# A gated-expert sum and a top-k attention laid over each other in one line of sixteen tiles

## The reference

```python
# end of block 0, _L0_ffn_ref: two gated experts' outputs of each token, projected and added
g = a * jax.nn.sigmoid(b)                       # 512 wide, per expert
eo = jnp.einsum('bth,dh->btd', g, Wo) + bo
out = out + eo * comb[..., e:e + 1]
...
# block 1, _L1_xattn_ref: 77 keys, 4 heads, the 32 largest scores of each
scores = jnp.einsum('bthd,bghd->bhtg', Q, K) / np.sqrt(DH).astype(np.float32)
topv, topi = jax.lax.top_k(scores, K_TOP)
probs = jax.nn.softmax(topv, axis=-1)
attn = jnp.zeros_like(scores).at[bi, hi, ti, topi].set(probs)
attn_mean = attn.mean(axis=1)
c_t = jnp.einsum('btg,bgd->btd', attn_mean, V)
x = layernorm(x_text, g_norm_in, b_norm_in)
scale_in, shift_in = jnp.split(c_t @ W_film_in + b_film_in, 2, axis=-1)
# x * (1 + scale) + shift (FiLM, mod_gate within) goes into a convolution over time (s4d), a second FiLM, a feed-forward network
```

## Time and profile before

| | |
|---|---|
| median of three runs | 844.28 us (844.15 to 856.82) |
| the profiled execution, its own time | 840.17 us |
| its span, first to last instruction | 838.1 us |
| busy share of the span | PE 81%, DVE 67%, POOL 46%, ACT 36% |
| mean granted TensorE clock | 0.905 of full speed |
| stage C | 398.2 to 594.8 us |
| gated sums start (their transposes) / top-k starts | 416.1 / 459.3 us |

### The profile page before, as it was taken

One profiled execution on the slowest core, in us unless ns is written; L12 is line 12 of the kernel. 1 busy time (PEld: TensorE's weight loads), 2 busy tenths in 40 slices (PEclk: granted clock), 3 DMA queues, 4 the chain that ended last, 5 costly groups with the idle time before them and its releaser, 6 DMA issues.

```text
span 838.1 us, 10777 instructions
## 1 busy us (share of the span) xinstructions
PE 677.0 (81%) x3380; PEld 378.6 (45%) x3380; DVE 564.4 (67%) x1711; ACT 303.2 (36%) x654; POOL 389.4 (46%) x450
## 2 busy tenths in 40 slices
PE   4779698449899999985898568767996999999971
PEld 2434455424354545442486223323442464657651
DVE  4868874667975656510677889988775595744266
ACT  2555564204546555510122535545211311031210
POOL 4979674037887879721102467886200120212020
PEclk9999998559999999988799779978897999999996
DMA  8920011202222222221980000200100000000003
GB/s 223 390 77 1 0 57 36 75 26 77 75 78 75 78 75 77 75 70 38 313 315 25 1 0 2 100 2 1 50 1 0 1 0 1 1 0 1 1 0 100
DMA packets 33087, 52.78 MB, mean 63 GB/s; under 512 B 8718, under 2 KB 21582, under 8 KB 32776
## 3 DMA queue, kind: packets, MB, share of 16 engines
q1 hardware_dynamic: 28040, 36.76, 13.1%
q0 software_dynamic: 4992, 15.34, 5.4%
HBM read 36.62 MB, written 15.47 MB: 62 GB/s over the span
## 4 chain that ended last, share of the span: by engine, by line
PE 44%; DVE 30%; POOL 9%; ACT 7%; issue 6%; DMA 2%; POOLq 1%; SPq 0%; DVEq 0%; ACTq 0%
PE ps L469 40%; DVE arena L1519 5%; DVE arena L2015 4%; POOL arena L1351 3%; DVE arena L2012 3%; POOL arena L1357 2%; DVE arena L335 2%; DVE kp L1519 2%; ACT L1145 1%; DVE arena L1871 1%; DVE arena L1522 1%; DVE arena L1525 1%; DVE arena L1622 1%; ACT arena L988 1%; DVE X L1525 1%
## 5 line engine op out<-in xcount | busy, mean ns | idle before, releaser
L469 PE MATMUL ps<-arena 64*32 64x32 f32 (+10 forms) x2344 | 495.8, 399 | 26.0 <-DVE arena L1808 8.7
L469 PEld LDWEIGHTS ps<-arena 64*32 64x32 f32 (+7 forms) x2344 | 233.7, 155 | 220.0 <-issue 171.4
L988 ACT ACTIVATE arena<-ps 128x512 f32<-128x512 f32 (+4 forms) x252 | 121.1, 493 | 283.3 <-PE ps L469 144.3
L330 POOL TENSOR_SCALAR rstd<-mv 128x1 f32<-128x1 f32 (+2 forms) x30 | 13.0, 434 | 234.4 <-DVE mv L324 183.4
L1871 DVE TENSOR_TENSOR arena<-ps,arena 128x512 f32<-128x512 f32 x39 | 26.9, 689 | 85.4 <-ACT arena L1145 77.4
L1400 POOL DMA_INDIRECT scr_g<-arena,destU x39 | 48.8, 1250 | 44.1 <-DVE arena L1871 35.3
L1391 POOL DMA_INDIRECT arena<-scr_z,idsU x39 | 49.5, 1270 | 22.8 <-PE ps L705 11.5
L2015 DVE MATCH_REPLACE8 arena<-arena 128x77 f32<-128x77 f32 x256 | 54.1, 222 | 0.0
L1145 ACT ACTIVATE arena<-ps 128x512 f32<-128x512 f32 x39 | 23.3, 598 | 83.6 <-PE ps L469 83.5
L1351 POOL TENSOR_TENSOR arena<-arena 128x616 f32<-128x616 f32 x32 | 40.2, 1257 | 20.7 <-DVE arena L1624 19.1
L1283 ACT ACTIVATE arena<-ps,b1p 128x512 f32<-128x512 f32 x32 | 22.0, 687 | 75.9 <-PE ps L469 75.9
(11 more groups left out here) (206 smaller groups left out, 1011.4 us busy)
## 6 DMA issues: line engine op xcount, KB each, us to landing
arena<-in_w1t SPq DMA_DIRECT2D x8, 1024.0 KB, 14.1
arena<-scr_g SPq DMA_DIRECT2D x8, 1024.0 KB, 7.9
X<-in_x SPq DMA_DIRECT2D x2, 1024.0 KB, 6.5
scr_z<-arena SPq DMA_DIRECT2D x4, 512.0 KB, 2.8
arena<-in_c_dftf SPq DMA_DIRECT2D x1, 2048.0 KB, 16.2
arena<-in_L_xattn_W SPq DMA_DIRECT2D x2, 1024.0 KB, 6.3
out<-X SPq DMA_DIRECT2D x16, 128.0 KB, 1.8
scr_k<-arena SPq DMA_DIRECT2D x4, 256.0 KB, 8.2
```

Of the source, the lines that this page charges most:

```text
L469: return pe.matmul(o, l, r, start=first, stop=final)
L988: return a.activation(o, i, ACT.Copy)
```

## The change

Parts 2 and 3 of stage C become one line. Six tiles (LEAD = 6) of the gated sums go ahead; then the attention of tile n runs together with the sum of tile n + 8, the turned sum of n + 7 and the projection of n + 6, on every engine.

What moves and changes:
- The first half of the gated sum (a scale per row) goes from VectorE to ScalarE (`half_sum`); loads come in eight pieces of two tiles in place of four of four, on four semaphores. Four of the eight are issued before the loads of the kernel rows and the Fourier table (KL, DF), four after them.
- The normalisation to U goes from VectorE to ScalarE, with mean and root combined to a bias (`nmrC`) on GpSimd, four tiles at a time.
- ScalarE also takes the exponentials of the rest `Rk`. TAKEN gives zero there, so all minus rest is the top 32. GpSimd does this subtraction, the scaling, and the sum of the four heads in two additions; VectorE's compare and reduce go away. `attn_ready` now comes from GpSimd.
- ScalarE scales the FiLM product by the root on its way out of PSUM (two copies of 256 in place of one of 512), and GpSimd's separate scale of U goes away.
- Banks: turned u, scores, projection, turned weights and FiLM product have one bank each in place of two for most. The turned sum keeps two.
- Input spectra go two per step in steps 11 to 14, in two banks. The bias additions to X come two per step in steps 8 to 15.

```diff
--- before.py
+++ after.py
...
+LEAD = 6
...
+        HALF = NSEL * 2 * HID0
+        yg = [Region(at).take(NSEL, 2, HID0) for at in
+              (0, HALF, keep_k + NT * D, keep_k + NT * D + HALF, keep_kl + 2048, keep_kl + 2048 + HALF, keep_k + NT * D + HALF)]
+        yg.append(kpf[:, 0:HALF].rearrange("p (a b c) -> p a b c", a=NSEL, b=2))
...
-                sp.wait_ge(s["gy0"], 32)
                 load_gated(2)
-                sp.wait_ge(s["gy1"], 32)
-                sp.wait_ge(s["sum_ready"], 4)
                 load_gated(3)
                 sp.wait_ge(s["k_out"], 64)
                 load(sp, KL, scr_k.rearrange("(k p) n -> p k n", p=P), "k_in")
                 load(sp, DF, d["c_dftf"].rearrange("(k p) n -> p k n", p=P), "dft_in")
+                for i in (4, 5):
+                    sp.wait_ge(s[f"gy{i - 4}"], 32)
+                    load_gated(i)
+                sp.wait_ge(s["gy3"], 32)
+                load_gated(7)
+                sp.wait_ge(s["gy2"], 32)
+                sp.wait_ge(s["sum_ready"], 8)
+                load_gated(6)
...
+                def out_B(T):
+                    pe.wait_ge(s["sumT_sb"], T + 1)
                     if T:
...
+                        pe.wait_ge(s["xB_done"], T)
+                    for f in range(4):
+                        ins = mm(ps[:, 4, 0:D], GT[:, T % 2, f, :], wof[:, f, :], f == 0, f == 3)
+                    ins.then_inc(s["oB_ps"], 1)
...
+                def film_in(n):
+                    pe.wait_ge(s["AT_sb"], n + 1)
+                    if n:
+                        pe.wait_ge(s["film_sb"], n)
+                    mm(bank(6), AT[0:BIAS_ROW + 1, n * P:(n + 1) * P], VW[0:BIAS_ROW + 1, n // TB, 0, :], True, True)\
+                        .then_inc(s["film_ps"], 1)
...
+                for T in range(LEAD + 1):
+                    turn_sum(T)
+                    if T:
+                        out_B(T - 1)
                 pe.wait_ge(s["prepC_v"], 7)
...
                 turn_u(0)
                 turn_u(1)
                 scores(0)
...
+                for n in range(NT + 1):
+                    if n + 1 < NT:
+                        scores(n + 1)
+                    if n + LEAD + 1 < NT:
+                        turn_sum(n + LEAD + 1)
+                    if n + LEAD < NT:
+                        out_B(n + LEAD)
+                    if 1 <= n <= 8:
+                        kernel_spectrum(n - 1)
+                    if n == 11:
+                        pe.wait_ge(s["sd_ready"], 2)
+                        pe.wait_ge(s["dfx_in"], 16)
+                        pe.wait_ge(s["ks_done"], 8)
+                    if 11 <= n <= 14:
+                        for i in (2 * (n - 11), 2 * (n - 11) + 1):
+                            if i >= 2:
+                                pe.wait_ge(s["xf_sb"], i - 1)
+                            spectrum(i // 2, i % 2, (5, 4)[i % 2])
+                    if n:
+                        turn_attn(n - 1)
+                    if n + 2 < NT:
+                        turn_u(n + 2)
+                    if n:
+                        film_in(n - 1)
...
+                def half_sum(T):
+                    i = T // 2
+                    a.wait_ge(s[f"gy{i % 4}"], 32 * (i // 4 + 1))
+                    if T >= 2:
+                        a.wait_ge(s["sumT_ps"], T - 1)
+                    a.activation(G[:, T % 2, :], yg[i][:, 0, T % 2, :], ACT.Copy, scale=cw[:, 0, T:T + 1])\
+                        .then_inc(s["gated_half"], 1)
...
+                def exp_top_and_rest(n):
+                    a.wait_ge(s["top_full"], n + 1)
+                    for h in range(H1):
+                        ins = a.activation(topx[:, n % 2, h, :], top[:, n % 2, h, :], ACT.Exp, bias=smC[:, n % 2, 3, h:h + 1],
+                                           accum_out=smC[:, n % 2, 0, h:h + 1])
+                    ins.then_inc(s["ex_sum"], 1)
+                    for h in range(H1):
+                        R_ = Rk[:, n % 2, h * S2:(h + 1) * S2]
+                        ins = a.activation(R_, R_, ACT.Exp, bias=smC[:, n % 2, 3, h:h + 1])
+                    ins.then_inc(s["rest_exp"], 1)
...
+                def put_film(n):
+                    a.wait_ge(s["film_ps"], n + 1)
+                    a.wait_ge(s["lnC_rstd"], 2 * (n // 4) + 2)
+                    if n >= 2:
+                        a.wait_ge(s["xin_ready"], n - 1)
+                    a.activation(filmS[:, n % 2, 0:D], bank(6, D), ACT.Copy, scale=rstd[:, TB + n:TB + n + 1])
+                    copy(filmS[:, n % 2, D:2 * D], ps[:, 6, D:2 * D]).then_inc(s["film_sb"], 1)
...
+                for T in range(LEAD + 1):
+                    put_sumT(T)
+                    half_sum(T + 2)
+                    if T == LEAD - 1:
+                        norm_u(0)
                 put_uT(0)
                 put_uT(1)
                 put_scores(0)
                 for n in range(NT + 1):
                     if n < NT:
...
+                        exp_all(n)
+                    if n + 1 < NT:
+                        put_scores(n + 1)
+                    if n + LEAD + 1 < NT:
+                        put_sumT(n + LEAD + 1)
+                    if n + LEAD + 3 < NT:
+                        half_sum(n + LEAD + 3)
+                    if 11 <= n <= 14:
+                        put_spectrum(2 * (n - 11))
+                        put_spectrum(2 * (n - 11) + 1)
+                    if n in (2, 6, 10):
+                        norm_u(n // 4 + 1)
+                    if n < NT:
+                        exp_top_and_rest(n)
+                    if 1 <= n <= 8:
+                        put_kernel(n - 1)
                     if n:
...
+                        put_attn(n - 1)
+                    if n + 2 < NT:
+                        put_uT(n + 2)
+                    if n:
+                        put_film(n - 1)
...
+                def weights(n):
+                    q_, E = smC[:, n % 2], Ex[:, n % 2, :]
+                    p.wait_ge(s["ex_sum"], n + 1)
+                    own.done(p.tensor_tensor(q_[:, 1, :], q_[:, 0, :], negone[:], ALU.pow))
+                    own.settle()
+                    own.done(p.tensor_scalar(q_[:, 2, :], q_[:, 1, :], tmask[:, n:n + 1], None, ALU.mult))
+                    p.wait_ge(s["rest_exp"], n + 1)
+                    own.done(p.tensor_tensor(E, E, Rk[:, n % 2, :], ALU.subtract))
+                    own.settle()
+                    hE = E.rearrange("p (h k) -> p h k", h=H1)
+                    own.done(p.tensor_tensor(hE, hE, q_[:, 2, :].unsqueeze(2).broadcast_to([P, H1, S2]), ALU.mult))
+                    own.settle()
+                    own.done(p.tensor_tensor(E[:, 0:2 * S2], E[:, 0:2 * S2], E[:, 2 * S2:SW], ALU.add))
+                    own.settle()
+                    if n >= 2:
+                        p.wait_ge(s["AT_ps"], n - 1)
+                    p.tensor_tensor(a77[:, n % 2, :], E[:, 0:S2], E[:, S2:2 * S2], ALU.add).then_inc(s["attn_ready"], 1)
+                def x_in(n):
+                    p.wait_ge(s["film_sb"], n + 1)
+                    F_, o = filmS[:, n % 2, :], XIN[:, n - n % 4 + XSLOT[n % 4], :]
+                    own.done(p.tensor_tensor(F_[:, 0:D], F_[:, 0:D], U[:, n, :], ALU.mult))
+                    own.settle()
+                    p.tensor_tensor(o, F_[:, 0:D], F_[:, D:2 * D], ALU.add).then_inc(s["xin_ready"], 1)
...
+                for n in range(NT + 2):
+                    if n in (2, 6, 10):
+                        rstd_u(n // 4 + 1)
+                    if n >= 2:
+                        x_in(n - 2)
+                    if 1 <= n <= NT:
+                        weights(n - 1)
+                    if n == 10:
                         p.wait_ge(s["ks_ps"], 8)
                         p.wait_ge(s["xin_ready"], TB)
                         for i, kind in enumerate((ALU.add, ALU.subtract)):
                             p.tensor_tensor(SD[:, i], *folded(0), kind).then_inc(s["sd_ready"], 1)
...
+                def add_B(T):
+                    v.wait_ge(s["oB_ps"], T + 1)
+                    v.tensor_tensor(X[:, T, :], X[:, T, :], ps[:, 4, 0:D], ALU.add).then_inc(s["xB_done"], 1)
+                    v.wait_ge(s["xB_done"], T + 1)
+                    own.done(v.bn_stats(bstat[:, T % TB, :], X[:, T, :]))
...
+                sum_gated(0)
+                sum_gated(1)
+                film_rows()
+                for T in range(LEAD):
+                    sum_gated(T + 2)
+                    add_B(T)
+                for n in range(NT):
+                    top_eight(n, 0)
+                    top_eight(n, 1)
+                    if n + LEAD + 2 < NT:
+                        sum_gated(n + LEAD + 2)
+                    top_eight(n, 2)
+                    if 2 <= n <= 9:
+                        kernel_pair(n - 2)
+                    top_eight(n, 3)
+                    if n + LEAD < NT:
+                        add_B(n + LEAD)
...
```

374 lines of the change are left out of this document (139 added, 235 removed).

## The result

The changed kernel takes 853.04 us (median of 20 executions) and the kernel before 844.65 us on the same chip. The ratio is 1.0116 with a 95% interval of 1.0097 to 1.0135: a small but sure loss of some 10 us (0.0116 x 844.65). The forecast was 846, with a range of 830 to 864. The profiled execution took 851.21 us, its span is 849.4. Some executions take 10 to 14 us more than the others of the same kernel; the ratios leave out those more than 1.5% above the fastest of their kernel, and the profiled executions of e2_fill and e6b_extras_after_weights are two of these.

The account below looks back on a forecast made before the run. The round trip through GpSimd, 8.4 us per tile, was taken as the bound, with TensorE's 8.85 in kernel-spectrum tiles. Stage D 3.3 us earlier plus 5 for clock gave 841.9 profiled; the median 4.1 above it, so 846, range 830 to 864.

Parts of the forecast that it names:

- tiles 9 and 10: Stage C loop: GpSimd's additions, statistics and folded sums make these tiles 11.2 and 12.0 us.
- The head start: Start of the stage C loop: first top-eight at 435 instead of 459.3, a gain of 24 us (21 to 26).
- Rival 3: Loop start: load behind the Fourier table, or single banks, hold the first top-eight until 440 or later; 851; chance 0.13.
- TensorE in the kernel tiles: Tiles with a kernel spectrum: 8.4 us of TensorE work, no faster than 8.85 us a tile, clock 1.00.
- Rival 2: Rewritten loop stays at the low clock: kernel tiles' 8.4 us become 11.1, about 862 in all; chance 0.17.
- The round trip: GpSimd's weights through turned weights, FiLM and x_in back to GpSimd's next weights: a cycle of 8.4 us per tile.
- the line: GpSimd's unmeasured widths: about 2.06 ns an element over 0.25 us, giving 0.86, 0.56 and 0.4 us.
- Rival 1: Stage C loop: VectorE is the bound and the cycle is hidden; 808 us; chance 0.12 with its softer form.
- Tiles 11 to 15: 5 x 8.4 = 42.0: End of the stage C loop: five tiles at the round trip's 8.4 us each, 42.0 us.
- the term of the clock: TensorE's low clock after idle time in tile 0 and tiles 9 and 10: +5 us, ends 0 and 20.
- ScalarE's work per tile, 6.6 us: Stage C loop: ScalarE's exponentials, copies and sums total 6.6 us per tile and fit under 8.4.
- norm before the second exponentials in tiles 2, 6, 10: An engine order counted as free; the prediction would be wrong if it delays the spectra. No size given.

Follow-up runs that it names:

- e2_fill: The changed kernel plus unread matmuls where TensorE waits (tile 0 and from step 9); ratio to the kernel before 1.0048, interval 0.9994 to 1.0101.
- e6b_extras_after_weights: Changed kernel with GpSimd's weights before input products, ScalarE's spectrum copies last, rstd behind weights, one wide fold in step 9; 0.9846 of the kernel before.
- e4: The changed kernel with LEAD 14 in place of 6, so the overlap is undone; ratio to the kernel before 1.0327.
- e3: The changed kernel with ScalarE's two input-spectrum copies in steps 11 to 14 moved to the end of the step; ratio to the kernel before 1.0014.
- e1: The changed kernel with GpSimd's weights(n-1) ahead of x_in(n-2) in each step; ratio to the kernel before 0.9981.
- e8: Changed kernel with GpSimd's weights before input products, ScalarE's spectrum copies last, and GpSimd's sixteen additions to X behind stage C; 0.9818 of the kernel before.

## Why the prediction was right, and which step was not

The time was in the range and within 2%, but 7 us above the forecast; on the profiled execution the sum was 841.9 and it took 851.21. By the prediction's own steps, from the first top-eight (D0):

| step | predicted | measured |
|---|---|---|
| first top-eight | 435 | 435.66 |
| weights of tile 8 | D0 + 87.1 | D0 + 90.1 |
| tiles 9 and 10 | 11.2 and 12.0 | 10.6 and 11.4 |
| tiles 11 to 15 | 42.0 | 52.0 |
| from there to stage D | 4.2 | 5.5 |
| stage D | D0 + 156.5 | D0 + 169.6 |
| all clock effects | +5, apart | in the rows above |

**The head start** was right, by the borders (37.2 us from the start of stage C to the first top-eight, in every overlapped trace) and by e4. Rival 3 is out.

**TensorE in the kernel tiles** was right: 8.8 us, busy 96%, clock 0.99. Rival 2 needed a mean clock of 0.77 there. The 3.0 us over at tile 8 were lost before the first kernel spectrum, at a granted clock of 0.62; in e3 the same stretch had 0.86, and the weights of tile 8 come at D0 + 86.9.

**The round trip** was right as a mechanism, and e1 shows it: take it away by order alone, and 11.4 us go. GpSimd's new operations were 0.2 us a tile cheaper than the line (which gives 0.88 at 308, not 0.86), inside their ends. The Trainium skill (GPSIMD Engine Reference, 4.1 Engine selection) puts a two-input elementwise operation on GpSimd at about twice VectorE's time. Here the subtract of 308 took 0.84 us where VectorE's compare of the same width took 0.53, 1.6 times, so its 1.05 was too dear. The rule's advice holds all the same: what moved cost more where it went. It isn't where the loss came from: e1 and e3 each undo most of it or all with the same operations on the same engines.

**Rival 1,** VectorE as the bound, was rightly put low: VectorE waited 36.5 us for GpSimd in this loop.

**The step that failed is "Tiles 11 to 15: 5 x 8.4 = 42.0"** and with it the term of the clock for "each of a few later tiles". The length of the round trip was right: with ScalarE's spectrum copies at the end of the step, the same five tiles take 42.5 us and the loop 156.8, against 42.0 and 156.5. What I missed is that in the order as written another ring is longer. The prediction added up ScalarE's work per tile, 6.6 us, and said that it fits under 8.4. It does, in the late tiles too (17.8 us of work in the 46 from 560 to 606); the sum says nothing on where in the list each piece stands. With two spectrum copies ahead of the top exponentials, a late tile is TensorE's spectra, then ScalarE's 3.0 us, one behind the other, and a low clock of TensorE goes straight to the end there. I had named an order that might cost ("norm before the second exponentials in tiles 2, 6, 10") and not the one next to it. The clock term of +5 covers half of the 10 us, so it was mis-sized as well, by not knowing that TensorE would be in the chain there. e3 shows the order's part. What the late tiles would take in the old order at the full clock stays an estimate (9.0 us), since e2's trace has the spectra at the same clock.

Signs that came as predicted: GpSimd idle before the first x_in product in 13 of 16 tiles and released by ScalarE; VectorE waiting at the start of tiles (2.8 us on average and up to 6.0, more than the 1 us I gave for a middle tile); tiles 9 and 10. Two sizes of ScalarE were off and cost nothing visible: the half sum 0.72 us (0.6, ends 0.5 and 0.7), the normalisation 0.49 us in a row of four (0.35, ends 0.3 and 0.5).

## What to carry to other kernels

When several engines run hand-written lists, add up each engine's work, and then walk the ring: for each result that an engine hands on, list what stands ahead of it in that engine's list and what those items wait for. An item that waits for a slow producer (a spectrum copy here, an input product there) belongs behind those that release others. Two swaps of order, with no work removed, turned a loss of 1.2% into a gain of 1.1%, and only then was it worth taking work off GpSimd, to 1.8%. A tile much longer than any engine's busy time in it points to a ring of waits; an engine's timeline without idle brackets is that of a full engine.

## What the runs showed that was not expected

**VectorE and GpSimd slow each other.** With GpSimd's 256-wide additions beside VectorE's 1024-wide products (e8), one of either took 1.64 us on average, where alone they take 0.73 and 1.22. The two have the same length, as if they took turns. The Trainium skill (SBUF — State Buffer, "Who interferes with whom") describes a port pair that the two engines share as an exclusive lock, and counts a VectorE operation with both inputs in SBUF among those that contend for it. The trace agrees that the two contend. Here both lose and go in step, and 1.64 is less than 0.73 + 1.22 = 1.95, so it looks as if part of an operation does run beside the other. In the changed kernel something like it shows where a gated sum meets an input product:

```profile
484.06 0.74 DVE L1622 SCALAR_TENSOR_TENSOR arena<-arena,cw 128x512 f32<-128x512 f32 x1
484.13 1.26 POOL L1558 TENSOR_TENSOR arena<-arena 128x256 f32<-128x256 f32 x1 [3.04 <-ACT arena L1011]
```

The product took 1.26 us and not 0.72. Another of the sixteen took 1.03 us, the other fourteen 0.72 to 0.79. The prediction had no term for it.

**A mean clock can rise without the work behind it going faster.** In e2's trace the window's clock went from 0.74 to 0.87, and the pieces of the chain kept their lengths, since the clock in them was the same. What counts is the clock while the chain's own matmuls run.
